# Attention pass of a graph network: whole f32 rows scattered by f32 products, and the table of dst read through a zero-padded tile

## The reference

```
h = (x @ W).reshape(n, HEADS, CH)
e = leaky_relu(a_src[src] + a_dst[dst], 0.2)
e = exp(e - segment_max(e, dst)[dst])
out = segment_sum(h[src] * (e / segment_sum(e, dst)[dst]), dst)
```

## Time and profile before

| | |
|---|---|
| median of 3 runs | 6627.94 us (6626.7 to 6636.36) |
| profiled execution | 6627.8 us, span 6625.9 us |
| PE, DVE, ACT, POOL busy | 76%, 74%, 56%, 19% of the span |
| mean granted TensorE clock | 0.869 of full |

### The profile page before, as it was taken

How to read it: one execution, slowest core, us unless ns; L and a number is a source line. 1 busy time by engine, 2 the same in 40 slices (tenths; PEclk the granted TensorE clock), 3 DMA queues, 4 the chain that set the end, 5 groups by cost and what they waited for, 6 DMA issues and landing times.

```text
span 6625.9 us, 249912 instructions
## 1 busy us (share of the span) xinstructions
PE 5019.0 (76%) x92226; PEld 3848.5 (58%) x92226; DVE 4884.0 (74%) x11072; ACT 3691.7 (56%) x10681; POOL 1287.5 (19%) x1884
## 2 busy tenths in 40 slices
PE   2666666655777777477759999968888887888887
PEld 1344444435666666366659999945555554555554
DVE  8999999988999999988875555555555555555554
ACT  3566666642333333344456666656666665666665
POOL 2455555543333333200000000000000000000000
PEclk7777777777777777688889999989999998999999
DMA  1000000005666666200003333322222222222222
GB/s 40 1 1 1 1 1 1 1 12 170 201 203 201 202 200 201 88 0 0 0 0 108 99 101 99 89 65 73 73 72 72 73 68 76 72 73 72 73 74 66
DMA packets 305206, 501.12 MB, mean 76 GB/s; under 512 B 76919, under 2 KB 78455, under 8 KB 305127
## 3 DMA queue, kind: packets, MB, share of 16 engines
q1 hardware_dynamic: 303782, 499.39, 26.2%
q0 software_dynamic: 576, 0.52, 0.0%
q10 hardware_dynamic: 768, 0.16, 0.0%
HBM read 408.40 MB, written 91.57 MB: 75 GB/s over the span
## 4 chain that ended last, share of the span: by engine, by line
issue 52%; DVE 24%; PE 15%; POOL 5%; DVEq 2%; ACT 1%; DMA 1%; POOLq 0%; ACTq 0%; SPq 0%
PE PS L1145 8%; DVE agg L1590 6%; POOL arena L625 5%; DVE arena L1554 4%; PE PS L1107 3%; DVE Hp L1554 3%; DVE arena L1596 2%; DVE tmp L1554 2%; PE PS L1203 1%; PE PS L1188 1%; PE PS L1152 0%; DVE arena L2137 0%; DVE arena L2147 0%; DVEq L1560 0%; DVE agg L2142 0%
## 5 line engine op out<-in xcount | busy, mean ns | idle before, releaser
L1554 DVE TENSOR_TENSOR arena<-iotab,arena 128x1024 bf16<-128x1024 bf16 (+6 forms) x1813 | 1752.5, 991 | 661.7 <-PE PS L1270 634.1
L882 ACT ACTIVATE arena<-PS 128x384 bf16<-128x384 f32 x2450 | 1176.3, 490 | 645.2 <-PE PS L1263 596.2
L1270 PE MATMUL PS<-arena 32*128 32x192 bf16 x41552 | 1245.5, 244 | 41.9 <-DVEq L2226 40.4
L746 ACT ACTIVATE arena<-PS,m 128x196 bf16<-128x196 f32 x1813 | 742.1, 427 | 548.0 <-POOLq L525 328.7
L1270 PEld LDWEIGHTS PS<-arena 32*128 32x128 bf16 x41552 | 762.0, 93 | 387.7 <-ACT arena L882 203.8
L1263 PE MATMUL PS<-Hp,arena 128*128 128x192 bf16 (+1 forms) x4900 | 813.6, 251 | 113.3 <-DMA arena<-hots 58.8
L1107 PE MATMUL PS<-Hp,arena 128*128 128x72 bf16 (+1 forms) x14700 | 812.1, 204 | 104.1 <-DVE arena L1920 40.8
L1107 PEld LDWEIGHTS PS<-Hp,arena 128*128 128x128 bf16 x14700 | 695.7, 102 | 132.1 <-DVE arena L1920 40.9
L995 PE MATMUL PS<-arena,tmp 128*128 128x262 bf16 x1813 | 508.2, 329 | 290.7 <-DVE tmp L1554 290.4
L863 ACT ACTIVATE arena<-PS,ewB 128x64 f32<-128x64 f32 x2450 | 532.8, 331 | 283.8 <-PE PS L1107 283.8
L987 PE MATMUL PS<-agg,onesb 128*128 128x196 bf16 x1715 | 516.2, 302 | 202.1 <-ACT arena L746 197.8
(11 more groups left out here) (349 smaller groups left out, 8047.0 us busy)
## 6 DMA issues: line engine op xcount, KB each, us to landing
arena<-hots SPq DMA_DIRECT2D x735, 256.0 KB, 2.7
arena<-codes SPq DMA_DIRECT2D x245, 512.0 KB
hots<-arena SPq DMA_DIRECT2D x245, 256.0 KB, 4.2
arena<-hots SPq DMA_DIRECT2D x147, 320.0 KB, 2.9
arena<-codes SPq DMA_DIRECT2D x49, 640.0 KB
hots<-arena SPq DMA_DIRECT2D x49, 320.0 KB, 4.5
rows_h<-Hn SPq DMA_DIRECT2D x4, 1568.0 KB, 8.9
rows_l<-Y SPq DMA_DIRECT2D x1, 1764.0 KB, 10.4
```

The costliest lines, as they stand in the source:

```text
L746: act.activation(junk[:, j % 4, :], ps[j % 4][:, 0:KEYS], ACT.Relu, bias=m256[:, 0:1], accum_out=rank[:, j:j + 1]).then_inc(k_rank, 1)
L882: act.activation(RG[g % 2][:, 2 * i:2 * i + 2, :].rearrange("p k c -> p (k c)"), ps[q % 2][:, 0:2 * RW], ACT.Copy).then_inc(r_ev, 1)
L1270: last = pe.matmul(ps[2 + q][:, b * RW:(b + 1) * RW], one_hot[32 * q:32 * q + 32, b * P:(b + 1) * P], rows_of[32 * q:32 * q + 32, :], star ...
L1554: return dve.tensor_tensor(to.rearrange("p k (n t) -> p k n t", t=4), iota_of[:, 0:n].rearrange("p (n t) -> p n t", t=4)[:, None, :, :] .t ...
```

## The change

1. **Scatter.** The split in three parts goes: `highest`, `middle`, `rest`, `lowest` and the tiles W3, Rf, W3m. Wf gets three buffers and is itself the moving operand, 68 f32 columns. OD becomes f32: DVE makes ODb in bf16 as before in two buffers, and ACT copies it to OD (`one_hots_whole`). OM is f32. The scatter is one f32 product per column, by the code that the weight pass uses too.
2. **Eviction.** One addition from PSUM in place of a reduction and an addition.
3. **Table of dst.** POOL fills two tiles `ztab` of 3 x 72 bf16 with zeros once, and before each window copies the 24 numbers of `tab` for it behind 64 zeros; PE's three products of 8 columns become three of 72 that read `ztab[b]`. PE waits for it once per window (`f_tab`).
4. **Loops.** Since b alternates, PE's loop holds two windows per pass (24 passes and a last window); the weight pass shares that loop. The one-hots of the weight pass lie elsewhere in the arena.

```diff
-        OD = [cv.take(GS[0] * P, bf16).rearrange("p (k n) -> p k n", n=P) for _ in range(3)]
-        W3 = [cv.take(GS[0] * W3W, bf16).rearrange("p (k c) -> p k c", c=W3W) for _ in range(2)]
+        ODb = [cv.take(GS[0] * P, bf16).rearrange("p (k n) -> p k n", n=P) for _ in range(2)]
+        OD = [cv.take(GS[0] * P).rearrange("p (k n) -> p k n", n=P) for _ in range(3)]
-        Wf = [cv.take(GS[0] * WV).rearrange("p (k c) -> p k c", c=WV) for _ in range(2)]
-        Rf = [cv.take(GS[0] * WV).rearrange("p (k c) -> p k c", c=WV) for _ in range(2)]
+        Wf = [cv.take(GS[0] * WV).rearrange("p (k c) -> p k c", c=WV) for _ in range(3)]
+        ztab = [cv.take(PARTS * WIDE, bf16).rearrange("p (a c) -> p a c", a=PARTS) for _ in range(2)]
...
+                def table_of(dx, b):
+                    if not (isinstance(dx, int) and dx < 2):
+                        pool.wait_ge(f_gath, dx * NG + (3 - NG))
+                        pool.sem_inc(s_held, 1)
+                    pool.tensor_copy(ztab[b][:, :, DIM:WIDE],
+                                     tab[:, bass.ds(dx * 24, 24)].rearrange("p (a c) -> p a c", a=PARTS)).then_inc(f_tab, 1)
+                for z in ztab:
+                    mlink(pool.memset(z, 0.0))
+                table_of(0, 0)
+                table_of(1, 1)
                 gather_few(Gm, t0, 0)
                 gather_few(Dm, td, 1)
-                for g in range(NG):
-                    lowest(0, 0, g, WV)
...
+                with pool.Fori(1, WINDOWS // 2) as i:
+                    table_of(i * 2, 0)
+                    table_of(i * 2 + 1, 1)
+                table_of(LASTW, 0)
...
             def exponents(dx, g):
                 act.wait_ge(f_mx, dx * NG + g + 1)
-                act.activation(Wf[g % 2][:, 0:GS[g], DIM:WV], mx[g % 2][:, 0:GS[g], :], ACT.Exp).then_inc(f_exp, 1)
+                act.wait_ge(f_scat, dx * NG + g + 1)
+                act.activation(Wf[g % 3][:, 0:GS[g], DIM:WV], mx[g % 2][:, 0:GS[g], :], ACT.Exp).then_inc(f_exp, 1)
+
+            def one_hots_whole(dx, g):
+                act.wait_ge(f_ohb, dx * NG + g + 1)
+                act.wait_ge(f_scat, dx * NG + g + 1)
+                act.activation(OD[g % 3][:, 0:GS[g], :], ODb[g % 2][:, 0:GS[g], :], ACT.Copy).then_inc(f_ohd, 1)
...
                     for g in range(NG):
-                        highest(0, dx, g, WV)
-                        middle(0, dx, g, WV)
                         if g < NG - 1:
                             exponents(dx, g + 1)
+                            one_hots_whole(dx, g + 1)
...
                         for a in range(PARTS):
-                            last = pe.matmul(to[:, DIM:WIDE], OT[g % 3][:, (sz + k) * P:(sz + k + 1) * P],
-                                             tab[:, bass.ds(dx * 24 + a * 8, 8)], start=False, stop=(a == PARTS - 1))
+                            last = pe.matmul(to[:, 0:WIDE], OT[g % 3][:, (sz + k) * P:(sz + k + 1) * P],
+                                             ztab[b][:, a, :], start=False, stop=(a == PARTS - 1))
...
-            def scatter(order, dx, g, v, used):
+            def scatter(order, dx, g, hot, rows_of, few, few_rows):
-                pe.wait_ge(f_low, n + (order * NN + 3))
+                pe.wait_ge(f_whole, n + (2 * order * NN + 3))
                 pe.wait_ge(f_ohd, n + (2 * order * NN + 1))
...
-                    last = pe.matmul(to, OD[g % 3][:, k, :], W3[g % 2][:, k, 0:used], start=(g % 3 == 0 and k == 0),
+                    last = pe.matmul(to, hot[g % 3][:, k, :], rows_of[g % 3][:, k, :], start=(g % 3 == 0 and k == 0),
...
-                with pe.Fori(0, LASTW) as d:
-                    body(d, False)
-                body(LASTW, True)
+                with pe.Fori(0, LASTW // 2) as i:
+                    body(i * 2, 0, False)
+                    body(i * 2 + 1, 1, False)
+                body(LASTW, 0, True)
...
-                    flink(dve.tensor_reduce(part[:, 0:v], got[:, 0:3 * v].rearrange("p (a c) -> p c a", a=PARTS),
-                                            AX.X, ALU.add))
-                    flink(dve.tensor_tensor(to, to, part[:, 0:v], ALU.add))
+                    flink(dve.tensor_tensor(to, to, ps[4 + h][:, 0:WV], ALU.add))
```

More of the change, by code:

```diff
@@ L246, in gnn_stack @@
         Wm = cv.take(MC * WV).rearrange("p (m c) -> p m c", m=MC)
-        W3m = cv.take(MC * W3W, bf16).rearrange("p (m c) -> p m c", m=MC)
+        ztab = [cv.take(PARTS * WIDE, bf16).rearrange("p (a c) -> p a c", a=PARTS) for _ in range(2)]
         cv = Carve()
-        cv.take(3 * 2 * GS[0] * P, bf16)
         w_OT = [cv.take(2 * GS[0] * P, bf16) for _ in range(3)]
@@ L1087, in _, with gather @@
             pe.sem_inc(f_scat, 3)
-            def gather(order, dx, g, attends):
+            def gather(order, dx, g, attends, b=0):
                 n = dx * NG + g
@@ L1131, in scatter @@
                     for m in range(MC):
-                        last = pe.matmul(to, OM[:, m, :], W3m[:, m, 0:used], start=False, stop=(m == MC - 1))
+                        last = pe.matmul(to, few[:, m, :], few_rows[:, m, :], start=False, stop=(m == MC - 1))
                     last.then_inc(f_sum, 1)
-            def scatter_whole(dx, g):
-                n = dx * NG + g
-                h = g // 3
-                to = ps[4 + h][:, 0:WIDE]
-                pe.wait_ge(f_whole, n + (2 * NN + 3))
-                pe.wait_ge(f_ohd, n + (2 * NN + 1))
-                if g % 3 == 0:
-                    pe.wait_ge(f_accout, dx * 2 + (2 * 2 * WINDOWS + h + 1))
-                for k in range(GS[g]):
-                    last = pe.matmul(to, w_OD[g % 3][:, k, :], Wq[g % 3][:, k, :], start=(g % 3 == 0 and k == 0),
-                                     stop=(g == 2 and k == GS[g] - 1))
-                last.then_inc(f_scat, 1)
-                if g == NG - 1:
-                    pe.wait_ge(f_misc, 3)
-                    pe.wait_ge(f_ohm, dx + (2 * WINDOWS + 1))
-                    for m in range(MC):
-                        last = pe.matmul(to, w_OM[:, m, :], w_Wm[:, m, :], start=False, stop=(m == MC - 1))
-                    last.then_inc(f_sum, 1)
@@ L1155, in edge_pass, with body @@
-            def edge_pass(order, v, used, attends):
-                def body(dx, last):
+            def edge_pass(order, attends, *tiles):
+                def body(dx, b, last):
                     for g in range(NG):
                         if g < NG - 2:
-                            gather(order, dx, g + 2, attends)
+                            gather(order, dx, g + 2, attends, b)
                         elif not last:
-                            gather(order, dx + 1, g + 2 - NG, attends)
-                        if attends:
-                            scatter(order, dx, g, v, used)
-                        else:
-                            scatter_whole(dx, g)
+                            gather(order, dx + 1, g + 2 - NG, attends, 1 - b)
+                        scatter(order, dx, g, *tiles)
@@ L1975, in evict @@
+                    for h in range(2):
+                        ks = slice(h * m, (h + 1) * m)
+                        last = dve.tensor_tensor(
+                            Wf[g % 3][:, ks, 0:DIM].rearrange("p k (h c) -> p k h c", h=HEADS),
+                            gathered_half(g, h)[:, :, 0:DIM].rearrange("p k (h c) -> p k h c", h=HEADS),
+                            bc(Wf[g % 3][:, ks, DIM:WV], CH), ALU.mult)
+                    last.then_inc(f_whole, 1)
                 def evict(dx, h):
@@ L1999, in body @@
                         weigh(dx, g)
-                        if attends and g < NG - 3:
+                        if g < NG - 3:
                             turned_one_hots(dx, g + 3)
-                        elif attends and not last:
+                        elif not last:
                             turned_one_hots(dx + 1, g + 3 - NG)
-                        rest(dx, g)
                         if g < NG - 1:
-                            if attends:
-                                scores(dx, g + 1)
+                            scores(dx, g + 1)
                             one_hots(dx, g + 1)
                         elif not last:
-                            if attends:
-                                scores(dx + 1, 0)
+                            scores(dx + 1, 0)
                             one_hots(dx + 1, 0)
@@ L2016, in body @@
                             few(dx)
-                            if attends and first:
+                            if first:
                                 dve.wait_ge(f_mmx, 1)
@@ L2024, in edge_pass @@
                 at[0], at[1] = ofs, 0
-                if attends:
-                    for g in range(3):
-                        turned_one_hots(0, g)
-                    scores(0, 0)
+                for g in range(3):
+                    turned_one_hots(0, g)
+                scores(0, 0)
                 one_hots(0, 0)
@@ L2084, in _ @@
             OFS = [0]
```

(2 more changed lines are left out.)

118 lines of the change are left out of this document (36 added, 82 removed).

## The result

| | before | after |
|---|---|---|
| median | 6627.32 us (6623.61 to 6636.36, 4 runs) | 6751.44 us (6748.53 to 6757.01, 4 runs) |
| profiled execution | 6627.8 us | 6750.44 us, span 6748.7 us |
| mean granted clock | 0.869 | 0.886 |

The ratio after to before is 1.0183, interval 1.0171 to 1.0196: 124 us slower, where 132 us faster was forecast. The time is outside the forecast range.

A forecast was written before the change was run, and what follows sets the result against it. DVE was taken to bound the attention pass at 24.39 us per window, the bound then moving to PE at 21.7 (16.4 + 50 x 0.106). Gain (24.39 - 21.7) x 49 = 132 us from 6627.8: 6496 us, range 6455 to 6610.

The forecast's parts named there:

- rival B: PE's doubled loop, attention pass: code loading at each jump back, 106 to 149 us more, 6602 to 6645; chance 0.13.
- The standing: PE at each jump back of the doubled loop: stands for a transfer, 2.7 to 4.5 us.
- The clock term: PE just after a jump's stand: half clock, 1.7 us lost, as after its wait for POOL's L625.
- A: Attention pass on PE: no gaps at clock 1.00, 21.7 us per window, 6496 us, own range 6448 to 6520; chance 0.67.
- column of the gather: PE's gather, attention pass: six products of 72 per column of edges take 0.193 us, bounds 0.173 to 0.196.
- The zeros up to 72: PE's table products, attention pass: the 64 zeros are nearly free, by the split of starts in the earlier trace.
- DVE: DVE, attention pass: rests, a reduction and eviction work go; 24.39 us per window falls to 17.0, an upper bound.
- L1895's gain: DVE's turned one-hots, formerly L1920: with POOL relieved, 4.6 us per window instead of 5.70, saves 1.1.
- ACT, POOL: Attention pass: ACT some 8 us per window, hidden by PE's work; POOL's one copy per window costed at nothing.
- Weight pass: Weight pass with its body written twice: zero change, PE covers it with no gap, 16.4 us per window.
- Rival C: PE's clock stays at 0.78 in the attention pass: 27.8 us per window, 167 slower, 6795 us; chance 0.12.
- Rival D: Hand-overs among PE, DVE and ACT take back part: 22.5 to 24 us per window, 6535 to 6610; chance 0.08.

The follow-up runs named there:

- experiment 3: Kernel before with only PE's shared loop doubled to two windows per pass: 6628.96 us, ratio 0.9994.
- experiment 4: experiment 2 with three windows per pass of PE's loop in the weight pass alone: 6441.99, 6442.37, 7200.05 and 7209.36 us.
- experiment 6: Changed kernel with 64 semaphore increments on PE ahead of the attention pass: 6505.24, 6504.77, 6549.4 and once 7722.23 us.
- experiment 9: Changed kernel with 112 semaphore increments on PE ahead of the attention pass: 6496.05 us, ratio 0.9779.
- experiment 5: Changed kernel with 192 semaphore increments on PE ahead of the attention pass: 6627.12 us, ratio 0.9966.
- experiment 1: Changed kernel with one zero tile instead of two and one window per pass of PE's loop: 6493.44 us, ratio 0.9796.
- experiment 2: Changed kernel with only the scatter's change: table products 8 wide straight from `tab`, no zero tile, single loop: 7198.08 us, ratio 1.0856.
- experiment 14: experiment 1 with table products of 8 columns, read from the zero tile: 7201.92 us, ratio 1.0838.
- experiment 7: experiment 1 with four windows per pass of PE's loop in the weight pass: 6664.6, 6715.96, 6786.93 and 6835.73 us.
- experiment 15: experiment 1 with table products of 24 columns: 6453.51 us, ratio 0.971; its profiled execution 6511.63 us.
- experiment 12: experiment 1 with table products of 40 columns: 6452.74 us, ratio 0.9728.

## Why the prediction was wrong, step by step

**What failed is rival B's weight and price.** B named the mechanism: a transfer at each jump back, then half clock. It stood at 0.13, and its price was 4.4 to 6.2 us per jump; measured were 6.1 of standing and 5.0 of clock, 11.1. Two terms were mis-sized. The standing was taken as one landing of 2.7 to 4.5 us, but there are two gaps per jump, 2.1 us (48.0/23) and 4.0 us (93.0/23) in the mean. The clock term was 1.7, taken from a short wait for POOL; after these gaps PE works 10 to 14 us at 0.50. Against that B counted 24 jumps where there are 23. With 23 x 11.1 = 256 us on A's 6496 the time is 6752; that is what put it above B's 6602 to 6645.

**B's chance rested on a comparison of lengths that doesn't decide.** The prediction said that 1038 loads and products cost nothing and left open whether 1624 would. Experiments 3, 4, 6 and 9 show loops of 1471, 1605 and even these 1676 instructions without a reload, and the changed kernel shows the 1676 reloaded with nine packets per jump. The number of blocks touched, seven or eight, fits the results of moves by 0, 64 and 112, and predicted the last; the place of the second gap in experiment 5 supports it. By that rule the reload of the changed kernel is an accident of where its loop starts. For the move of 192 the rule gives a reload, but not why only part of the passes had one. The Trainium skill ("Runtime: NRT & Kernel Launch", section "Instruction fetch mechanics") gives PE 2048 instructions in blocks of 256. Eight blocks are just that; the runs agree with the block of 256, and they put the usable length at seven blocks. Why nine are loaded where eight are touched is not shown. The same section also says that only two blocks are held and that a taken branch beyond them stalls; loops of six and seven blocks ran here without any packet more, so for a loop the measurement decides against that.

**The sum of A: right.** Window 21.74 against 21.7; column of the gather 0.196 us, the upper end of 0.173 to 0.196 (0.193 was taken); f32 records 0.1137, the same for 68 columns as for 72; experiment 1 gave 6493, experiment 9 gave 6496, the forecast was 6496. The zeros up to 72 are not nearly free, as I had read from the earlier trace rows: a window with 24 or 40 columns is 1.05 us shorter, 0.021 per column of edges, so that such a column costs 0.175, near the 0.173 of before. The Trainium skill ("TensorE: Matmul & The Clock Gate", "Wait — 56ns, not 53.3ns?") gave 0.195 for six products of 72, and the trace agrees.

**DVE, right.** Rests and reductions are gone, the eviction L1936 takes 0.217 us (0.223 forecast), L1895 takes 0.743 us with a maximum of 0.90 in place of the 1.29 of the earlier trace rows. DVE works 14.9 us per window at full rate; 17.0 was called an upper bound. That POOL's leaving brought L1895's gain fits, but no run kept POOL busy beside the new kernel, so it is argued, not shown.

**ACT, POOL, right.** L798 takes 1.058 us (1.023 forecast), ACT 7.9 us per window (8). POOL's copy (0.74 us) is waited for once for 0.6 us in experiment 1.

**Weight pass, right.** PE busy 770 of 770 us at 1.00 with a doubled body.

**Rival C, wrongly weighed in its reasons.** The changed kernel left 0.78 for 1.00 between jumps, as A said. But that the weight pass has 1.00 with the same f32 products was no argument: the same f32 scatter with the old 8-wide table products sits at 0.50 all through the pass (experiments 2, 14). The zero columns, which the prediction costed only as added work, are what gives this pass its clock in nearly every execution. My reason "a slow PE is a busier PE, so gaps close" was true and no help: PE has no gap at all in experiment 2, and is still at 0.50.

**Rival D, no sign.** No wait for L1924 or ACT of any size.

## What to carry to other kernels

Before a loop body of PE is doubled, compare the packets of the instruction queue with the program's length, afterwards too: an excess per pass of the loop means that the code is loaded again, and moving the loop's start by a fraction of 256 instructions, or one window per pass, can take all of it away. A stand of PE of some three microseconds cost about twice its length in the attention pass and far more in the weight pass of experiment 7, so price it with the clock behind it, and take the price from the pass where it falls. And where a full PE shows 0.50, try making small products in it wider before looking for a wait.

## What the runs showed of the hardware that was not expected

- PE busy 500 of 500 us stays at 1.2 GHz in one kernel and at 2.4 GHz in another that differs only in the width of the three table products per column of edges, 8 against 24 numbers: 36.13 against 20.70 us per window. The same code took both courses (experiment 4), and a full PE was at 0.50 for 140 us at the start of the weight pass in one execution and for under 40 in another (experiments 15 and 12). What decides between them is open.
- A loop of 1676 instructions was reloaded or not by a shift of 64 or 112 instructions: 6751 against 6505 and 6496 us. Nine blocks came in at a jump that missed, none at the others.
- A reload comes as two gaps with one microsecond of work between them in the changed kernel, and as one gap of some 2.4 to 4.0 us in experiment 7. In both the first gap comes 32 instructions behind the jump.
- Standing of 3.5 us was followed by half clock that cost 4.2 us; 6.1 us in two gaps by 5.0; 2.7 us in the weight pass by some 17.
- f32 products of 68 and 72 columns cost the same, 0.1137 us per record at 1.00, and, for 68 columns, 0.216 at 0.50.
